# Three PSUM pairs in turn for slots and ranks, gather rows worked out by POOL, and one reduction for each half of the gathered rows

## The reference, cut to what matters

```python
def _L0_gnn_ref(A, X, W, b):
    mask = A != 0
    scores = jnp.where(mask, -jnp.arange(N), -jnp.inf)
    vals, idx = jax.lax.top_k(scores, S)             # the first 25 neighbours of each row
    valid = vals > -jnp.inf
    feats = jnp.where(valid[..., None], X[idx], -jnp.inf)
    agg = feats.max(axis=2)
    agg = jnp.where((degree <= S)[..., None], jnp.maximum(agg, 0.0), agg)
    return relu(concat([X, agg]) @ W + b)

x = x + _L0_gnn_ref(adj, _layernorm(x), ...)         # x: 8 images x 1024 rows x 128
x = x + _L0_ffn_ref(_layernorm(x), ...)              # two hidden layers of 256, shared + routed expert, residual
```

## Time and profile before

| | |
|---|---|
| median of 3 runs | 740.54 us (737.5 to 740.84) |
| profiled execution | 736.18 us, its span 734.5 us |
| PE busy | 611.5 us (83%) |
| DVE busy | 574.2 us (78%) |
| ACT busy | 521.2 us (71%) |
| POOL busy | 541.9 us (74%) |
| slot matmuls (L777), PE | 375.5 us |
| slot folds (L988), DVE | 293.7 us |
| mean granted clock of TensorE | 0.926 |

### The profile page before, as it was taken

How to read it: one execution, slowest core, us unless ns; L and a number is a source line. 1 busy time by engine, 2 the same in 40 slices (tenths; PEclk the granted TensorE clock), 3 DMA queues, 4 the chain that set the end, 5 groups by cost and what they waited for, 6 DMA issues and landing times.

```text
span 734.5 us, 11755 instructions
## 1 busy us (share of the span) xinstructions
PE 611.5 (83%) x3496; PEld 502.9 (68%) x3497; DVE 574.2 (78%) x959; ACT 521.2 (71%) x981; POOL 541.9 (74%) x388
## 2 busy tenths in 40 slices
PE   0466666679999799979997999899987999799686
PEld 0054545566987588858885888668875988588565
DVE  3766799878987898779987898789878987777740
ACT  5672455369977898779876987699769985478062
POOL 4577488497979987898878897989799878984000
PEclk9986798898999899979998999989998999799989
DMA  9999997479746965496638755785474543045222
GB/s 298 305 196 265 314 344 241 134 176 293 226 132 158 267 175 152 102 259 205 166 109 222 236 163 142 190 240 159 127 182 124 161 138 87 22 113 144 58 72 77
DMA packets 145171, 131.73 MB, mean 179 GB/s; under 512 B 72219, under 2 KB 112324, under 8 KB 145092
## 3 DMA queue, kind: packets, MB, share of 16 engines
q1 hardware_dynamic: 128124, 105.94, 53.5%
q0 software_dynamic: 7296, 15.74, 8.3%
q10 hardware_dynamic: 9680, 9.21, 4.5%
HBM read 98.20 MB, written 17.98 MB: 158 GB/s over the span
## 4 chain that ended last, share of the span: by engine, by line
PE 59%; DVE 22%; issue 5%; DVEq 4%; DMA 4%; ACT 4%; SPq 1%; ACTq 0%
PE slot_ps L777 28%; PE ffn_ps L842 11%; DVE acc L988 9%; PE ffn_ps L852 4%; PE ffn_ps L826 4%; PE prep_ps L869 3%; DMA at<-mask 2%; PE ffn_ps L811 2%; PE ffn_ps L792 2%; DVEq L1060 2%; DVE top L1047 2%; PE ffn_ps L812 2%; DMA adj_sb<-in_adj_dram 2%; DVE wst L1153 1%; DVE score L1049 1%
## 5 line engine op out<-in xcount | busy, mean ns | idle before, releaser
L777 PE MATMUL slot_ps<-onehot,xsplit 128*128 128x512 f32 (+3 forms) x1376 | 375.5, 401 | 51.1 <-DVE acc L988 44.4
L988 DVE TENSOR_TENSOR acc<-slot_ps,acc 128x896 f32<-128x896 f32 (+2 forms) x336 | 293.7, 884 | 77.3 <-PE slot_ps L777 74.5
L547 POOL TENSOR_SCALAR onehot<-rank,ranks 128x896 fp32r<-128x896 bf16 (+3 forms) x128 | 298.4, 2333 | 72.6 <-PE slot_ps L777 67.5
L777 PEld LDWEIGHTS slot_ps<-onehot,xsplit 128*128 128x128 f32 x1376 | 251.9, 204 | 105.7 <-issue 71.0
L535 POOL DMA_INDIRECT gath<-feature_table,idx x200 | 207.7, 1038 | 47.9 <-issue 42.6
L842 PE MATMUL ffn_ps<-hT,wst 128*128 128x128 f32 x1024 | 135.1, 277 | 0.0
L842 PEld LDWEIGHTS ffn_ps<-hT,wst 128*128 128x128 f32 x1024 | 129.0, 191 | 5.9 <-issue 0.8
L670 ACT ACTIVATE away<-rank,ranks 128x896 bf16<-128x896 bf16 (+4 forms) x136 | 107.9, 793 | 6.8 <-DVE wst L1153 6.4
L687 ACT ACTIVATE onehot<-away 128x896 fp32r<-128x896 bf16 (+4 forms) x136 | 96.3, 708 | 21.5 <-PE slot_ps L777 10.6
L629 ACT ACTIVATE hT<-ffn_ps,wst 128x128 f32<-128x128 f32 x256 | 81.1, 375 | 29.5 <-PE ffn_ps L842 27.3
L641 ACT ACTIVATE rank<-prep_ps 128x448 bf16<-128x448 f32 x128 | 63.0, 550 | 21.0 <-PE prep_ps L869 11.7
(11 more groups left out here) (121 smaller groups left out, 586.3 us busy)
## 6 DMA issues: line engine op xcount, KB each, us to landing
wst<-folded_weights SPq DMA_DIRECT2D x128, 257.0 KB, 2.9
adj_sb<-in_adj_dram SPq DMA_DIRECT2D x64, 512.0 KB, 5.9
folded_weights<-wst ACTq DMA_DIRECT2D x34, 256.0 KB, 6.9
hT<-in_L_ffn_Wr_dram SPq DMA_DIRECT2D x26, 256.0 KB, 10.3
xs<-in_x_dram SPq DMA_DIRECT2D x8, 512.0 KB, 8.1
feature_table<-xn SPq DMA_DIRECT2D x8, 512.0 KB, 4.1
x<-in_x_dram SPq DMA_DIRECT2D x8, 512.0 KB, 4.3
out_dram<-h SPq DMA_DIRECT2D x16, 256.0 KB, 2.4
```

What stands on the lines that cost most here:

```text
L547: pool.tensor_scalar(onehot[:, UNIT[n]:UNIT[n] + many, 0:wide * P], rank[:, b % 2, first:first + many, 0:wide * P], ranks[:, r - 1:r], Non ...
L777: mm = pe.matmul(slot_ps[n % 2][:, c0:c1], xsplit[:, b % 2, part, first + j, :], onehot[:, UNIT[n] + j, c0:c1], start=(j == 0 and part == ...
L988: dve.tensor_tensor(acc[:, p % 2, 0:cols], slot_ps[n % 2][:, 0:cols], acc[:, p % 2, 0:cols], ALU.max).then_inc(s_max, 1)
```

## The change

- `slot_ps` becomes three pairs; `prep_ps` is gone. A new function, `bank_ring`, lists slots and ranks in program order and gives each the pair of the item three back. PE waits for that item: for DVE's fold if it was a slot, for ACT's read if it was a rank (`free_pair`).
- A rank is one item: 512 and 384 columns into one pair, one read of 896 columns by ACT.
- DVE's folds of slots 2 to 43 wait for the fold two back themselves.
- POOL works out the rows to gather, at p = 30 (17 in stage 0), with four operations; before, DVE did it at p = 28. The gathers start at 31 and end at 25 of the next stage.
- The maximum over the gathered rows is two tensor_reduce operations (13 rows; 12 rows and the first result) at p = 14 and 31 (26 and 36 in stage 1), instead of trees in four pieces.
- The one-time transposes of small weights use `ffn_ps`.

```diff
-CHUNKS = 2
+BANKS = 3
...
-    REDUCE_AT = {14: (0, 0, 0), 24: (0, 0, 1), 31: (0, 1, 0), 34: (0, 1, 1)}
-    FIRST_REDUCE_AT = {26: (0, 0, 0), 27: (0, 0, 1), 36: (0, 1, 0), 37: (0, 1, 1)}
+    REDUCE_AT = {14: (0, 0), 31: (0, 1)}
+    FIRST_REDUCE_AT = {26: (0, 0), 36: (0, 1)}
...
-    GATHER_AT = {29: [0], 30: [1], 32: [2], 33: [3], 35: [4], 36: [5], 38: [6], 39: [7], 41: [8], 42: [9]}
-    GATHER_NEXT = {0: [10], 1: [11], 3: [12], 5: [13], 6: [14], 8: [15], 10: [16], 12: [17], 13: [18],
-                   15: [19], 17: [20], 19: [21], 20: [22], 22: [23], 24: [24]}
+    ROWS_AT = [17, 30]
+    GATHER_AT = {31: [0], 32: [1], 34: [2], 35: [3], 37: [4], 38: [5], 40: [6], 41: [7], 43: [8]}
+    GATHER_NEXT = {0: [9], 2: [10], 3: [11], 5: [12], 7: [13], 8: [14], 10: [15], 12: [16], 13: [17], 15: [18],
+                   17: [19], 18: [20], 20: [21], 22: [22], 23: [23], 25: [24]}
...
-        slot_ps = [pb(f"slot_ps{i}", [P, 2 * BANK]) for i in range(2)]
-        prep_ps = [pb(f"prep_ps{i}", [P, 1024], BF16) for i in range(2)]
+        slot_ps = [pb(f"slot_ps{i}", [P, 2 * BANK]) for i in range(BANKS)]
...
+        def bank_ring():
+            pair, last, order = {}, {}, []
+            for s, p in positions():
+                if 1 <= s <= B:
+                    order.append(("slot", (s - 1) * NS + p))
+                if s < B and p in RANK_AT[s > 0]:
+                    order.append(("rank", s * IT + RANK_AT[s > 0][p]))
+            for m, item in enumerate(order):
+                pair[item] = m % BANKS
+                last[item] = order[m - BANKS] if m >= BANKS else None
+            return pair, last
...
+            def rows_to_gather(s):
+                pool.wait_ge(s_top, TOPS * (s + 1))
+                if s >= 2:
+                    pool.wait_ge(s_hub, HUBS * (s - 1))
+                pool.tensor_scalar(spread[:, :], top[:, 0, 0:TOPK], 0.0, lane[:, 0:1], ALU.is_equal, ALU.mult
+                                   ).then_inc(s_rows, 1)
+                pool.tensor_scalar(floor[:, s % 2, 0:1], top[:, 0, TOPK:TOPK + 1], 0.0, NEG_BIG, ALU.is_gt, ALU.mult
+                                   ).then_inc(s_rows, 1)
+                pool.wait_ge(s_rows, 4 * s + 2)
+                pool.tensor_tensor(spread[:, :], spread[:, :], top[:, 0, 0:TOPK], ALU.subtract).then_inc(s_rows, 1)
+                pool.wait_ge(s_rows, 4 * s + 3)
+                pool.tensor_scalar(idx[:, s % 2, 0, :], spread[:, :], float(N), None, ALU.add).then_inc(s_rows, 1)
+                pool.wait_ge(s_rows, 4 * s + 4)
...
-                    for c in range(CHUNKS):
-                        act.wait_ge(s_rank, 2 * IT * s + 2 * jt + c + 1)
...
-                        act.activation(rank[:, s % 2, jt, c * CW:(c + 1) * CW], prep_f[c][:, 0:CW],
-                                       ACT.Copy, bias=float(NONE)).then_inc(s_q, 1)
+                    act.wait_ge(s_rank, IT * s + jt + 1)
...
+                    act.activation(rank[:, s % 2, jt, :], slot_ps[PAIR["rank", s * IT + jt]][:, 0:COLS],
+                                   ACT.Copy, bias=float(NONE)).then_inc(s_q, 1)
...
+            def free_pair(item):
+                if LAST_IN[item]:
+                    kind, i = LAST_IN[item]
+                    if kind == "slot":
+                        pe.wait_ge(s_max, i + 1)
+                    else:
+                        pe.wait_ge(s_q, i + 1)
+                return slot_ps[PAIR[item]]
...
-                if n >= 2:
-                    pe.wait_ge(s_max, n - 1)
+                to = free_pair(("slot", n))
...
+                    to = free_pair(("rank", s * IT + jt))
+                    for c0 in range(0, COLS, BANK):
+                        cols = slice(c0, min(c0 + BANK, COLS))
+                        mm = pe.matmul(to[:, cols], before[:, :], at[:, jt, cols], start=True, stop=not second)
                         if second:
...
+                            mm = pe.matmul(to[:, cols], onesb[:, :], at[:, jt - 1, cols], start=False, stop=True)
+                    mm.then_inc(s_rank, 1)
...
             def fold_slot(b, p):
                 n = b * NS + p
                 cols = SLOTS[p][2] * P
+                if p >= 2:
+                    dve.wait_ge(s_max, n - 1)
                 dve.wait_ge(s_slot, n + 1)
...
-                if p == TOP_AT[s > 0][-1] + 1:
-                    rows_to_gather(s)
...
+            def reduce_half(b, h, part):
 
                 n = b * HUBS + h + 1
...
+                if part == 0:
                     dve.wait_ge(s_gathA, 16 * HALF * n)
...
+                    if n > 1:
+                        dve.wait_ge(s_redB, n - 1)
+                    dve.tensor_reduce(gath[:, TOPK, :], gath[:, 0:HALF, :].rearrange("p k c -> p c k"), AX_X, ALU.max
+                                      ).then_inc(s_redA, 1)
+                else:
                     dve.wait_ge(s_gathB, 16 * (TOPK - HALF) * n)
...
+                    dve.wait_ge(s_redA, n)
+                    dve.tensor_reduce(half_max[:, :], gath[:, HALF:TOPK + 1, :].rearrange("p k c -> p c k"), AX_X,
+                                      ALU.max).then_inc(s_redB, 1)
+                    dve.wait_ge(s_redB, n)
+                    dve.wait_ge(s_rows, 4 * n)
```

More of the change, by code:

```diff
@@ L69, in gnn_ffn_program @@
     COLS = TT * P
-    CW = COLS // CHUNKS
     HID = Wi.shape[0]
@@ L543, in one_hot @@
                 if p == min(q for q in POOL_HOT if SLOTS[q][0] == g):
-                    pool.wait_ge(s_q, 2 * IT * b + 2 * (first + many))
+                    pool.wait_ge(s_q, IT * b + first + many)
                 if FREE[n] > 0:
@@ L566, in _ @@
                     one_hot(n)
+                if s < B and p == ROWS_AT[s > 0]:
+                    rows_to_gather(s)
                 if 0 < s < B and p == SPLIT_AT:
@@ L665, in distance @@
                 i = b * len(SQUARED) + SQUARED.index(p)
-                act.wait_ge(s_q, 2 * IT * b + 2 * (first + 1))
+                act.wait_ge(s_q, IT * b + first + 1)
                 if i >= AWAYS:
@@ L679, in one_hot @@
                 if r == 1:
-                    act.wait_ge(s_q, 2 * IT * b + 2 * (first + many))
+                    act.wait_ge(s_q, IT * b + first + many)
                     act.activation(onehot[:, UNIT[n]:UNIT[n] + many, 0:wide * P],
@@ L776, in slot @@
                             c1 = min(c0 + BANK, wide * P)
-                            mm = pe.matmul(slot_ps[n % 2][:, c0:c1], xsplit[:, b % 2, part, first + j, :],
+                            mm = pe.matmul(to[:, c0:c1], xsplit[:, b % 2, part, first + j, :],
                                            onehot[:, UNIT[n] + j, c0:c1], start=(j == 0 and part == 0),
@@ L859, in prepare @@
                     second = [f for f, many in GROUPS if many == 2 and f + 1 == jt]
-                    for c in range(CHUNKS):
-                        if jt == 0:
-                            for i, many in enumerate(turns((s + 1) * TT)):
-                                pe.wait_ge(s_turn[i], 16 * many)
-                            if s > 0:
-                                pe.wait_ge(s_q, 2 * IT * s - 1 + c)
-                        else:
-                            pe.wait_ge(s_q, 2 * IT * s + 2 * jt + c - 1)
-                        cols = slice(c * CW, (c + 1) * CW)
-                        mm = pe.matmul(prep_f[c][:, 0:CW], before[:, :], at[:, jt, cols],
-                                       start=True, stop=not second)
+                    if jt == 0:
+                        for i, many in enumerate(turns((s + 1) * TT)):
+                            pe.wait_ge(s_turn[i], 16 * many)
@@ L896, in _ @@
                     pe.wait_ge(s_above, 1)
-                    pe.matmul(prep_f[0][0:1, 0:ROWS], above[:, 0:1], ident[0:ROWS, 0:ROWS], start=True,
+                    pe.matmul(slot_ps[0][0:1, 0:ROWS], above[:, 0:1], ident[0:ROWS, 0:ROWS], start=True,
                               stop=True).then_inc(s_overs, 1)
@@ L971, in one_hot @@
                 if p == min(q for q in DVE_HOT if SLOTS[q][0] == g):
-                    dve.wait_ge(s_q, 2 * IT * b + 2 * (first + many))
+                    dve.wait_ge(s_q, IT * b + first + many)
                 if FREE[n] > max(0, n - DVE_AHEAD + 1):
@@ L985, in fold_slot @@
                 if p < 2:
-                    dve.tensor_scalar(acc[:, p, :], slot_ps[n % 2][:, 0:cols], 0.0, None, ALU.max).then_inc(s_max, 1)
+                    dve.tensor_scalar(acc[:, p, :], slot_ps[PAIR["slot", n]][:, 0:cols], 0.0, None, ALU.max).then_inc(s_max, 1)
                 else:
-                    dve.tensor_tensor(acc[:, p % 2, 0:cols], slot_ps[n % 2][:, 0:cols], acc[:, p % 2, 0:cols],
+                    dve.tensor_tensor(acc[:, p % 2, 0:cols], slot_ps[PAIR["slot", n]][:, 0:cols], acc[:, p % 2, 0:cols],
                                       ALU.max).then_inc(s_max, 1)
@@ L1043, in top_piece @@
                 r, what = divmod(n // HUBS - 1, 2)
+                if n == HUBS and s > 0:
+                    dve.wait_ge(s_rows, 4 * s)
```

(4 more changed lines are left out.)

70 lines of the change are left out of this document (14 added, 56 removed).

## The result

The changed kernel takes 756.7 us (754.7 to 759.7), the median of four runs, where the kernel before takes 740.7: 16.0 us or 2.2% more. The ratio on record is 1.027, 95% interval 1.023 to 1.030; the two medians by themselves give 1.022, the spans of the two profiled executions, 753.7 us against 734.5, give 1.026, and the listed times do not explain the difference. By each of them the change is slower. Forecast were 725.1 us; the result is above the third rival's 747.5 as well.

The account below looks back on a forecast made before the run. PE bounds most of a pass, DVE slots 8 to 12, single late folds slots 31 and 0. Terms 2.8 + 4.9 - 1.5 + 5.4 + 3.8 = 15.4 us take 740.5 to 725.1 us; range 717 to 731.

Parts of the forecast that it names:

- the third rival: Reductions at slots 14 and 31 read spread elements at half speed, 3.5 us each: slower, 747.5 us; chance 0.10.
- One reduction a half: DVE at slots 14 and 31: one reduction takes 1.88 us, no surcharge for elements 512 bytes apart, no stall.
- The third pair, slots 8 to 13: Slot 13 starts 1.5 us earlier; ScalarE's copy lets PE keep 0.4 a pass, 2.8 us over seven passes.
- Slot 0: Start of the next image: PE's wait of 0.46 us for a fold goes; 0.7 us a pass, 4.9 us.
- Slot 39: Behind a rank, PE waits for ScalarE's whole read of 896 columns: 0.25 us lost in six passes, -1.5 us.
- Rows on POOL: Slot 31: without DVE's row operations fold 29 starts earlier, PE's wait goes; 0.9 us in six passes, 5.4 us.
- First pass: DVE is the chain PE waits for, so savings on reductions and row operations count in full: 3.8 us.
- Rival 1, ScalarE,: ScalarE, waited for more often, gives gains at slots 0 and 31 back at slots 25 and 39: 732; chance 0.17.
- Rival 2, the clock,: PE's gains at the banks are lost to longer low-clock stretches, nothing measurable: 738; chance 0.10.
- Sum: Whole kernel: 2.8 + 4.9 - 1.5 + 5.4 + 3.8 = 15.4 us saved.

Follow-up runs that it names:

- e1: The kernel before with one part only: each half reduced in one instruction, after slots 14 and 31; 758.2 us, ratio 1.033.
- e5: The changed kernel with its two reductions reading contiguous elements, so maxima of other numbers; 729.0 us, ratio 0.990.
- e14: The changed kernel with its first reduction reading elements 24 bytes apart, the second 16 bytes; 758.9 us.
- after: The changed kernel itself, with the whole change, against the kernel before; 756.7 us, ratio 1.027.
- e8: The kernel before with the three-pair ring alone, and gather 16 on POOL one step earlier, ahead of its slot 15 one-hot; 722.6 us, ratio 0.980.
- e3: The kernel before with the ring of three pairs alone, tree and rows on DVE kept; 738.1 us, ratio 1.003.
- e4: The kernel before with only the rows worked out on POOL and the gathers moved to their new places; 732.3 us, ratio 0.995.
- e7: The changed kernel with the tree back, and gather 15 on POOL one step earlier, ahead of its slot 15 one-hot; 722.1 us, ratio 0.980.
- e10: e7 with one-step reductions in the first pass only; ratio 0.982 to the kernel before.
- e9: The changed kernel, reductions kept after slots 14 and 31, with gather 15 on POOL one step earlier; 744.9 us, ratio 1.013.

## Why the prediction was wrong, point by point

**One reduction a half: the step that failed.** "The only spread reads in the trace are short ... so I take no surcharge" was the choice. The term was 1.88 us; it measured 3.08, which is past the 2.9 us from which the third rival was to decide, and that rival is what happened (e1, e5). At 1664 elements the surcharge is 1.2 us or 0.7 ns an element (e14: 0.8 at 24 bytes), which would be some 12 ns in 16 elements. The row that the choice rested on could have shown that much: its six executions at 24 bytes took 175 to 178 ns, the contiguous ones 175 to 184. It shows none, so it was read rightly; but it is a row of another operation, a tensor_tensor of two inputs, and a hundred times shorter, and what it shows does not carry over to a long tensor_reduce. Which of the two makes the difference, the operation or the length, no run here tells. The Trainium skill (Advanced Engine Details and Errata, SBUF Cachelines) says that lines are of 16 bytes and that at least two hits on a line are needed to absorb the latency. The reductions agree: 8 bytes, two reads a line, free; 16 bytes, one read, 1.68 times the time (3.158 / 1.875). The short row does not. The prediction knew the rule and gave its rival a chance of 0.10; against one row of another operation it should have had much more.

**Rival 3's size.** It gave 747.5 at 3.5 us a reduction; 3.08 gave 756.7. Two terms were missing in it. The hub's operation, pushed into POOL's one-hot, takes 1.48 us in the six middle passes where before it took 0.41 in five of them: 1.1 us a pass. And it took the 1.5 us that the third pair was to give at slot 14 as cover; that lead was not there.

**The third pair, slots 8 to 13.** "DVE's own work does not shrink here, so the folds stay where they are" failed: I held DVE's folds fixed, while DVE's one-hot for slot 13 (in every second pass of after the step on 16 numbers too) and POOL's for slot 15 run side by side, and which one pays differs from kernel to kernel. In the pass of the table it cost the lead of 2.4 us at slot 10 and 1.7 more. That "what is late next is ScalarE" proved right once the collision was gone (e8: 0.97 us at the first matmul after slot 14), and ScalarE's chain left PE nothing at slot 15 (0.03), not 0.4. The Trainium skill has a rule for this, which the prediction cited for the rows (SBUF — State Buffer, Who interferes with whom): the one that issues first holds the shared ports for the whole instruction. The trace agrees in e3 (3.80 us for DVE, 2.55 for POOL), and only in part in after, as said under the last heading. I applied it where the change removes an operation and did not look for the next pair of operations that it would bring together.

**Slot 0.** Right: slot 43 to slot 0 takes 0.83 us instead of 1.44 in each of the seven, 0.6 (said 0.7).

**Slot 39.** Right in after: 1.40 instead of 1.20 us behind slot 38, 0.2 (said 0.25). In five passes of e8, where PE runs further ahead, it is 1.84 to 1.89. ScalarE's read of 896 columns takes 0.93 us (said 1.0).

**Rows on POOL.** Right in place and size: slot 31 comes 2.62 us after slot 30 before and 1.70 in after and e4, 0.92 (said 0.9). POOL's four operations take 0.24 to 0.43 us each, 1.3 us from first to last (said 2). But the gain is not the rows' alone: with the ring and the rows still on DVE (e3, e8) slot 31 is as early. It then waits for no fold at all. Either part removes that wait, so as a part of the whole change the rows were worth less than 5.4 us; e7 and e8 differ by nothing.

**First pass.** 4.3 us shorter in the profile (said 3.8), but that pass takes 102 to 106 us from kernel to kernel for reasons that stay open (e10), so it does not confirm the step; at the 1.88 us of the forecast (e5) it would have been 7.5 us shorter, twice what was said. Not in the sum at all: the first stage ends 3.2 us earlier in after (slot 0 at 36.3, not 39.5), and in every kernel with the ring (35.5 to 36.4), in none without (38.7, 39.4). The eight ranks follow one another over three pairs there, which is the likely cause; no run tests it. I had looked at the ring only from slot 0 on.

**Rival 1, ScalarE,** did not decide: no wait of PE for a rank copy appears in after, e3 or e7, and one of 0.3 us in e8.

**Rival 2, the clock,** did not decide: the mean granted clock is 0.923 in after, 0.926 before, 0.932 in e7. My estimate from these means and the spans is 116 us at the lower of the two levels in after and 109 before, so at most 3 or 4 us of the loss, and that may as well be its effect.

**Sum.** Of what was forecast, slot 0 gave some 4 us and slot 31 5.5; the ring's start, which was not, gave 3.2. Against these 13 us stand the collision (e9 to after: 1.4%, 10 us) and the reductions (e7 to e9: 3.3%, 24 us): 21 us slower, where 16 to 20 were measured. The first pass, 4 us shorter in after than before, is not in this count.

## What to carry to other kernels

Before folding a tree of element-wise maxima into one strided reduction, price it at the pitch it will have: from a pitch of 16 bytes on the reduction cost 1.85 to 1.97 ns an element, at 4 and 8 bytes 1.13, and with the tree's contiguous steps the kernel was 3.3% faster (e9 to e7). Give the long instruction the place where the engine that is waited for has slack; the same 3 us cost 1.8 and 2.5 us of PE's time at two places and 0.9 and 0.6 at two others. And when a change lets one engine run ahead, list the pairs of DVE and GpSimd instructions that overlap or begin within a microsecond of each other, before and after: the third pair was worth nothing (1.003) until one gather was moved, and 2% with it.
